# Output projection of the cross attention from split operands, split during the attention

## The chip, the cores and the metric

The program runs on one core of one Trainium2 chip. The metric is the device time of one execution in microseconds (us). Before the change the median of three runs is 2769.53 us (2766.48 to 2770.44).

## What is computed

The reference is one transformer block over x (2 x 512 tokens of 512 features): a cross attention of 16 heads against a context of 2 x 8192 tokens, a window attention, and a mixture of 16 experts with a shared feed-forward part. The change touches the last line of the first part:

```python
    out = jnp.einsum('bhqk,bhkd->bhqd', scores, v)
    out = out.transpose(0, 2, 1, 3).reshape(b, -1, N_HEADS * D_K)
    return out @ Wo.T + bo          # 1024 x 512 times 512 x 512
x = x + _L0_xattn_ref(_layernorm(x), ctx_1024, ctx_1024, mask, Wq, bq, ..., Wo, bo)
```

All of it is in fp32, and the output has to be nearly as exact as fp32.

## The kernel before, in words

TensorE takes a fp32 operand in two ways here. As plain fp32, where the profile shows two matmul records for each product, or as fp32r, a rounded form, where it shows one. Where the kernel wants the speed of fp32r and the exactness of fp32 it splits each operand: high = the operand rounded to fp32r (a ScalarE copy), low = operand minus high (a VectorE subtraction), and the product is the sum of three fp32r products, high*high, high*low and low*high. The projections of keys and values (L1896, L1908), the products of the middle stage (L1001) and those of the experts (L712, L759) are made so. The output projection (L261) is not: it multiplies plain fp32.

The program has four stages: the projection of the context in 32 chunks (to about 741 us), the attention (to 1800 us), a middle stage with the output projection, the window attention, the gate and the shared feed-forward part, and the experts.

**The attention** goes through 8 groups bg, each a batch and four heads, stacked on 128 partitions; a group goes through 64 tiles of 128 keys. For a tile TensorE makes four score products of 128 x 512 into a ring of six PSUM banks (`score`, L433), seven products ahead of their use; ScalarE takes the exponential into one of six buffers PR (`attention_scalar`, L515 one bank at a time, L519 two at a time: of the eight banks of two tiles, four go one by one and four as two pairs, so that two tiles are four L515 and two L519); TensorE multiplies by the values into bank 7 (`values`, L444); VectorE adds the tile's exponentials to one of two sums AC (`attention_vector`, L548 for the first four tiles, L552 for the others). Tiles 13, 27, 41 and 55 (`KEPT`) are not added by VectorE: TensorE multiplies them by ones (`kept_sums`, L458). A group's denominator is completed by TensorE from AC in the fifth tile of the next group (`denominator`, L460). ScalarE waits before it overwrites a buffer PR until VectorE has added the tile six before (`buffer_free`, L493). When a group is done, ScalarE copies its output from PSUM to AT (`copied_out`, L489, called at u % 128 == 2 of the next group); VectorE takes the reciprocal of the denominator and multiplies (`normal`, L528, after the eighth tile of the next group).

GpSimd does nothing in the attention: `attention_gpsimd` (L415) has two memsets, which run at 728 us. SyncE loads keys, values and queries, and WO, the output weights of 1 MB, once, at the third chunk (`attention_sync`, L400).

**The end of the attention.** The output projection has eight tiles of 128 tokens, wo0 to wo3 for batch 0 and wo4 to wo7 for batch 1, each the sum of four products over the groups of its batch (`output_projection`, L256). wo0 and wo1 come before the last group's denominator (L482, L483), wo2 and wo3 behind it; the last group belongs to batch 1, so wo4 to wo6 wait until it is normal (L1095), then come four transposes of tokens (`turn`, t20 to t23, L991), then wo7. An order written out by hand (`ORDER`, L222) gives each result one of four PSUM banks in turn: `claim` waits until the bank's last content has been taken. wo4 takes the bank of wo0, t21 to t23 those of wo4 to wo6, wo7 that of t20. VectorE takes them in this order (`middle_vector`, L1378): adds wo0 to wo3 to X with statistics between (L1388, L1391), normalises those four tiles (L1401 to L1413, with one step on GpSimd, L977), adds wo4 to wo6, subtracts for the low halves of the four transposed tiles (L1421), adds wo7. The first product of the window attention (k00, L1104) is behind wo7 on TensorE. SyncE starts to load the window weights when the last group is normal (`middle_sync`, L903).

SBUF: AT and WO are plain views of AT_R and WO_R at the same addresses. The tiles of the attention are given back at L560, and those of the middle stage take their place.

Of the kernel before, what the change touches and what calls it, by code (L numbers as in the profile page):

```python
# [22 lines left out]
F32 = mybir.dt.float32  # L23
F32R = mybir.dt.float32r
I32 = mybir.dt.int32
U32 = mybir.dt.uint32
ALU = mybir.AluOpType
ACT = mybir.ActivationFunctionType
AX = mybir.AxisListType

P = 128
B, SQ, D = 2, 512, 512
# [3 lines left out]
G = D // P  # L36
# [6 lines left out]
BG = B * G  # L43
# [25 lines left out]
def program(nc, x, ctx_t, mask, wq, bq, wk, bk, wv, bv, ident_d, blocks_d, wo, bo, pre, bqkv, wlat, blat_c,  # L69
            blat_r, wmask_d, wproj, bproj, gate_w, up_w, gw, down_w, bias_d, pick_d, sh_down, out):  # L70
    st = ExitStack()
    with st:
        def sem(name):
            return st.enter_context(nc.semaphore(name))
# [15 lines left out]
        PS = st.enter_context(nc.psum_tensor("PS", [P, 8, 512], F32))  # L90
# [40 lines left out]
        with ExitStack() as plain:  # L131
            AT = plain.enter_context(nc.sbuf_tensor("AT", [P, BG, SQ], F32))
            WO = plain.enter_context(nc.sbuf_tensor("WO", [P, G, D], F32))
# [53 lines left out]
        with ExitStack() as s1:  # L187
            def sb(name, shape, dt=F32):
                return s1.enter_context(nc.sbuf_tensor(name, shape, dt))
# [66 lines left out]
        def output_projection(pe, i):  # L256

            b, q = divmod(i, TT // B)
            bank = claim(pe, f"wo{i}")
            for g in range(G):  # L260
                m = pe.matmul(PS[:, bank, :], AT[:, g * B + b, q * P:(q + 1) * P], WO[:, g, :],  # L261
                              start=(g == 0), stop=(g == G - 1))
            m.then_inc(s_full[bank], 1)

        s_wo = sem("output_weights_in")
        s_s, s_exp, s_pv, s_acc, s_l, s_o, s_rec, s_norm = (sem(n) for n in (
            "scores_ready", "exp_ready", "tile_values_added", "sums_added",
            "denominator_ready", "output_copied", "reciprocal_ready", "output_normal"))
        GT = NCH * KT
# [44 lines left out]
        PR = [sb(f"PR{i}", [P, J, SQ]) for i in range(BUFS)]  # L314
        AC = [[sb(f"AC{x}{h}", [P, J, SQ]) for h in range(2)] for x in range(2)]
        RC = sb("RC", [P, SQ])

        def exact_max_sync(sp):
            with sp.If(sp.value_load(flag[0:1, 0:1]) == 0):
# [74 lines left out]
        def attention_sync(sp):  # L394
            for N in range(1, BG * NCH):
                bg, n = divmod(N, NCH)
                if N == 2:
                    for s in range(2):
                        sp.wait_ge(s_kvst[s], STORES * NC_ALL // 2 + 1)
                    sp.dma_start(WO[:], wo).then_inc(s_wo, 16)  # L400
                if n == 0:
                    if bg >= 2:
                        sp.wait_ge(s_s, (bg - 1) * J * GT)
                    load_queries(sp, bg % 2, bg)
                if N >= 2:
                    sp.wait_ge(s_s, (N - 1) * J * KT)
                if N >= 2:
                    load_keys(sp, N % 2, N, bg % B * NCH + n)
                if N >= 2:
                    sp.wait_ge(s_pv, (N - 1) * KT)  # L410
                else:
                    sp.wait_ge(s_vps, 2 * KT + NC_ALL * KT)
                load_values(sp, N % 2, N)

        def attention_gpsimd(pool):  # L415
            pool.wait_ge(s_kps, NC_ALL * G)
            nc.gpsimd.memset(KS[1][3 * DH:P].bitcast(F32), 1.0).then_inc(s_row, 1)
            nc.gpsimd.memset(QS[1][3 * DH:P].bitcast(F32), 0.0).then_inc(s_row, 1)

        def attention_tensor(pe):  # L420
            def score(m):
                tile, j = divmod(m, J)
                N, t = divmod(tile, KT)
                bg = tile // GT
                if m % (J * GT) == 0:
                    pe.wait_ge(s_qs[bg % 2], (bg // 2 + 1) * QSB)
                if m % (J * KT) == 0:
                    pe.wait_ge(s_kv[N % 2], (N // 2 + 1) * KVB)
                if m >= RING:
                    pe.wait_ge(s_exp, exponentials(m - RING))  # L430
                elif m >= G:
                    pe.wait_ge(s_vs, NC_ALL * KT + m - G + 1)
                pe.matmul(PS[:, m % RING, :], KS[N % 2][:, j, t * P:(t + 1) * P], QS[bg % 2][:, j, :],  # L433
                          start=True, stop=True).then_inc(s_s, 1)

            def values(tile):
                bg, q = divmod(tile, GT)
                N, t = divmod(tile, KT)
                if t == 0:
                    pe.wait_ge(s_v[N % 2], (N // 2 + 1) * 16)  # L440
                if q == 0 and bg:
                    pe.wait_ge(s_o, bg)
                for j in range(J):
                    m = pe.matmul(PS[j * DH:(j + 1) * DH, OUTB, :], VC[N % 2][:, t, j * DH:(j + 1) * DH],  # L444
                                  PR[tile % BUFS][:, j, :], start=q == 0, stop=q == GT - 1)
                m.then_inc(s_pv, 1)

            def column_sums(src, start=False, stop=False):

                for j in range(J):  # L450
                    m = pe.matmul(PS[j * DH:(j + 1) * DH, SUMB, :], ones[:], src[:, j, :], start=start, stop=stop)  # L451
                return m

            def kept_sums(bg, q):

                if q == KEPT[0] and bg:
                    pe.wait_ge(s_rec, bg)
                column_sums(PR[(bg * GT + q) % BUFS], start=q == KEPT[0]).then_inc(s_l, 1)  # L458

            def denominator(bg):  # L460

                pe.wait_ge(s_acc, (bg + 1) * MARKS)
                column_sums(AC[bg % 2][0])
                column_sums(AC[bg % 2][1], stop=True).then_inc(s_l, 1)

            for m in range(LEAD):
                score(m)
            pe.wait_ge(s_vs, (NC_ALL + 1) * KT)
            for p in range(BG * GT // 2):
                bg, q = divmod(2 * p, GT)  # L470
                for m in range(p * BATCH + LEAD, min((p + 1) * BATCH + LEAD, NM)):
                    score(m)
                pe.wait_ge(s_exp, 8 * p + 8)
                values(2 * p)
                values(2 * p + 1)
                if q + 1 in KEPT:
                    kept_sums(bg, q + 1)
                if bg and q == 4:
                    denominator(bg - 1)
            pe.wait_ge(s_wo, 16)  # L480
            pe.wait_ge(s_norm, BG - 1)
            output_projection(pe, 0)  # L482
            output_projection(pe, 1)  # L483
            denominator(BG - 1)
            output_projection(pe, 2)
            output_projection(pe, 3)

        def attention_scalar(act):
            def copied_out(bg):  # L489
                act.wait_ge(s_pv, bg * GT + GT)  # L490
                nc.scalar.activation(AT[:, bg, :], PS[:, OUTB, :], ACT.Copy).then_inc(s_o, 1)

            def buffer_free(tile):  # L493

                act.wait_ge(s_pv, tile + 1)
                bg, q = divmod(tile, GT)
                if q in KEPT:
                    act.wait_ge(s_l, summed(bg, q))
                else:
                    act.wait_ge(s_acc, added(tile))  # L500

            act.wait_ge(s_vps, 2 * KT + NC_ALL * KT)
            act.wait_ge(s_vs, (NC_ALL + 1) * KT)
            for i in range(2):
                act.wait_ge(s_qst[i], 32 * (BG // 2))
                act.wait_ge(s_pst[i], 16 * SLICES + 1)
            for u in range(NM // 2):
                tile, hp = divmod(u, 2)
                bank = 2 * u % RING
                if hp == 0 and tile >= BUFS:  # L510
                    buffer_free(tile - BUFS)
                if halved(u):
                    for jj in range(2):
                        act.wait_ge(s_s, 2 * u + jj + 1)
                        nc.scalar.activation(PR[tile % BUFS][:, 2 * hp + jj], PS[:, bank + jj, :], ACT.Exp,  # L515
                                             scale=SCALE).then_inc(s_exp, 1)
                else:
                    act.wait_ge(s_s, 2 * u + 2)
                    nc.scalar.activation(PR[tile % BUFS][:, 2 * hp:2 * hp + 2], PS[:, bank:bank + 2, :], ACT.Exp,  # L519
                                         scale=SCALE).then_inc(s_exp, 2)  # L520
                if u % (2 * GT) == 2 and u >= 2 * GT:
                    copied_out(u // (2 * GT) - 1)
            copied_out(BG - 1)

        def attention_vector(dve):
            v = nc.vector
# [26 lines left out]
                    if bg and i == 7:  # L553
                        normal(bg - 1)
            normal(BG - 1)
            dve.wait_ge(s_norm, BG)

# [342 lines left out]

        def middle_sync(sp):  # L903
            sp.wait_ge(s_norm, BG)
            for i in range(2):
                sp.wait_ge(s_pst[i], 16 * SLICES + 1)

# [76 lines left out]
        def middle_tensor(pe):  # L984
# [107 lines left out]
                                  start=(f == 0), stop=(f == FS - 1))  # L1092
                m.then_inc(s_full[bank], 1)

            pe.wait_ge(s_norm, BG)  # L1095
            for i in range(4, TT - 1):
                output_projection(pe, i)
            for i in range(4):
# [992 lines left out]
```

## Time and profile before

| what | value |
|---|---|
| median of three runs | 2769.53 us |
| profiled execution, its own time | 2769.25 us |
| its span (first to last instruction) | 2767.5 us |
| TensorE busy, share of the span | 2741.3 us, 99% |
| VectorE / ScalarE / GpSimd busy | 2197.8 / 1736.6 / 88.9 us |
| instructions | 38269 |

Times of a row are microseconds from the start of the span unless marked ns. PE is TensorE's matmul, PEld its weight load, DVE VectorE, ACT ScalarE, POOL GpSimd, SPq SyncE's DMA queue. L552 is line 552 of the kernel. A matmul is pipelined, so the mean time of one is longer than the step from one to the next. A bracket behind a row gives the time for which the engine was idle before it and what ended that.

### The profile page before, as it was taken

The page shows a single profiled execution, that of the slowest core. Times are in us where ns is not written, and L with a number is a line of the kernel's source. Part 1 is how long each engine was busy: PE and PEld are TensorE (multiplying, and loading weights), DVE is VectorE, ACT ScalarE, POOL GpSimd, SP SyncE. Part 2 cuts the span into 40 slices and gives each one's busy share as a digit, 9 for nine tenths or more (in the row PEclk, how much of TensorE's full clock was granted, in tenths as well). Part 3 has the DMA queues.
Part 4 walks back from the last instruction along what each step waited for, and adds up shares of the span by engine and source line. Part 5 has one row for each costly group of instructions (what it writes and reads, how often), then busy time and mean ns, then how long its engine had stood idle before and what let it go on. Part 6 is the DMA issues. An engine that isn't in the chain of part 4 may idle for free.

```text
span 2767.5 us, 38269 instructions
## 1 busy us (share of the span) xinstructions
PE 2741.3 (99%) x14389; PEld 1811.2 (65%) x14389; DVE 2197.8 (79%) x1645; ACT 1736.6 (63%) x2519; POOL 88.9 (3%) x43
## 2 busy tenths in 40 slices
PE   9999999999999999999999999999999999999998
PEld 5888888888744444444444444457766788888886
DVE  6545544445599999999999999967659888888886
ACT  4222222222499999999999999916531577777775
POOL 0000000000000000000000000000000400000000
PEclk9999999999999999999999999999999999999999
DMA  6666666666655555556555565430352899999995
GB/s 232 231 229 235 228 217 233 235 227 235 193 127 141 132 135 134 140 127 141 128 138 137 133 142 131 109 106 32 122 195 91 326 360 349 343 353 345 347 345 195
DMA packets 245283, 553.30 MB, mean 200 GB/s; under 512 B 19971, under 2 KB 85891, under 8 KB 215805
## 3 DMA queue, kind: packets, MB, share of 16 engines
q1 hardware_dynamic: 241548, 542.91, 61.3%
q0 software_dynamic: 3584, 8.39, 1.4%
q8 instruction: 94, 1.54, 0.2%
q14 instruction: 57, 0.46, 0.1%
HBM read 423.10 MB, written 128.12 MB: 199 GB/s over the span
## 4 chain that ended last, share of the span: by engine, by line
PE 97%; DVE 1%; DMA 1%; issue 0%; ACT 0%; POOL 0%; SPq 0%; DVEq 0%; ACTq 0%
PE PS L433 19%; PE PS L444 17%; PE PS L1908 13%; PE PS L1896 12%; PE PS L712 12%; PE PS L759 6%; PE PS L1001 6%; PE PS L1091 2%; PE PS L451 1%; PE PS L701 1%; PE PS L261 1%; PE PS L1951 1%; PE PS L1059 1%; PE PS L738 1%; PE PS L1024 1%; DMA RAW<-in_gw 1%
## 5 line engine op out<-in xcount | busy, mean ns | idle before, releaser
L552 DVE TENSOR_TENSOR AC<-AC,PR 128x2048 f32<-128x2048 f32 x448 | 988.5, 2282 | 4.8 <-ACT PR L515 4.8
L515 ACT ACTIVATE PR<-PS 128x512 f32<-128x512 f32 x1024 | 567.6, 610 | 64.7 <-PE PS L433 42.0
L433 PEld LDWEIGHTS PS<-QS,KS 128*128 128x128 f32 x2048 | 364.0, 187 | 333.1 <-ACT PR L519 182.4
L433 PE MATMUL PS<-QS,KS 128*128 128x512 f32 x2048 | 562.7, 415 | 0.8 <-ACT PR L519 0.5
L519 ACT ACTIVATE PR<-PS 128x1024 f32<-128x1024 f32 x512 | 502.4, 1051 | 0.0
L444 PE MATMUL PS<-PR,VC 128*32 128x512 f32 x4096 | 492.5, 598 | 0.7 <-ACT PR L515 0.7
L610 DVE TENSOR_TENSOR WL<-RAW,WH 128x2048 fp32r<-128x2048 f32 x192 | 436.4, 2287 | 60.2 <-ACT WH L605 60.2
L1828 ACT ACTIVATE KH<-PS,bk_s 128x512 fp32r<-128x512 f32 x128 | 88.0, 690 | 520.2 <-PE PS L1896 520.2
L605 ACT ACTIVATE WH<-RAW 128x2048 fp32r<-128x2048 f32 x192 | 362.0, 1913 | 11.6 <-PE PS L1091 5.2
L1713 DVE SCALAR_TENSOR_TENSOR KL<-PS,bk_s,KH 128x512 fp32r<-128x512 f32 x128 | 95.5, 750 | 258.4 <-ACT KH L1828 258.4
L444 PEld LDWEIGHTS PS<-PR,VC 128*32 128x32 f32 x4096 | 106.8, 109 | 216.5 <-issue 169.2
L712 PE MATMUL PS<-WL,XEH 128*128 128x512 f32 x512 | 200.5, 392 | 0.0
L712 PE MATMUL PS<-WH,XEL 128*128 128x512 f32 x512 | 200.1, 391 | 0.0
L712 PE MATMUL PS<-WH,XEH 128*128 128x512 f32 x512 | 199.6, 390 | 0.0
L1908 PE MATMUL PS<-WVH,CL 128*128 128x512 f32 x512 | 199.3, 389 | 0.1
L1908 PE MATMUL PS<-WVH,CH 128*128 128x512 f32 x512 | 199.4, 389 | 0.0
L1908 PE MATMUL PS<-WVL,CH 128*128 128x512 f32 x512 | 199.2, 389 | 0.0
L1896 PE MATMUL PS<-CH,WKH 128*128 128x512 f32 x496 | 192.9, 389 | 0.0
L1896 PE MATMUL PS<-CL,WKH 128*128 128x512 f32 x496 | 192.9, 389 | 0.0
L1896 PE MATMUL PS<-CH,WKL 128*128 128x512 f32 x496 | 192.9, 389 | 0.0
L1722 DVE TENSOR_TENSOR VS<-PS,bv_s 128x512 f32<-128x512 f32 x128 | 85.2, 686 | 84.5 <-PE PS L1908 84.5
L800 ACT ACTIVATE HTH<-PS 128x512 fp32r<-128x512 f32 x64 | 38.3, 599 | 146.8 <-PE PS L738 146.8
(244 smaller groups left out, 3366.7 us busy)
## 6 DMA issues: line engine op xcount, KB each, us to landing
KS<-kh_d SPq DMA_DIRECT2D x256, 256.0 KB
RAW<-in_gw SPq DMA_DIRECT2D x64, 1024.0 KB, 6.2
RAW<-in_up_w SPq DMA_DIRECT2D x64, 1024.0 KB, 5.7
RAW<-in_down_w SPq DMA_DIRECT2D x64, 1024.0 KB, 5.6
kh_d<-KH SPq DMA_DIRECT2D x32, 1024.0 KB, 4.4
kl_d<-KL SPq DMA_DIRECT2D x32, 1024.0 KB, 6.5
v_d<-VS SPq DMA_DIRECT2D x128, 256.0 KB, 2.9
KS<-kl_d SPq DMA_DIRECT2D x128, 256.0 KB
```

The costliest lines, as they stand in the source:

```text
L433: pe.matmul(PS[:, m % RING, :], KS[N % 2][:, j, t * P:(t + 1) * P], QS[bg % 2][:, j, :], start=True, stop=True).then_inc(s_s, 1)
L444: m = pe.matmul(PS[j * DH:(j + 1) * DH, OUTB, :], VC[N % 2][:, t, j * DH:(j + 1) * DH], PR[tile % BUFS][:, j, :], start=q == 0, stop=q == ...
L515: nc.scalar.activation(PR[tile % BUFS][:, 2 * hp + jj], PS[:, bank + jj, :], ACT.Exp, scale=SCALE).then_inc(s_exp, 1)
L519: nc.scalar.activation(PR[tile % BUFS][:, 2 * hp:2 * hp + 2], PS[:, bank:bank + 2, :], ACT.Exp, scale=SCALE).then_inc(s_exp, 2)
L552: v.tensor_tensor(a[i % 2][:], a[i % 2][:], p[:], ALU.add).then_inc(s_acc, 1)
L605: nc.scalar.activation(WH[n % PAIRS][:], RAW[:, n % RAWS], ACT.Copy).then_inc(s_hi, 1)
L610: nc.vector.tensor_tensor(WL3[n % PAIRS][:], RAW[:, n % RAWS], WH[n % PAIRS][:].bitcast(F32), ALU.subtract).then_inc(s_lo, 1)
L712: m = pe.matmul(PS[:, bank, :], x[e % 2][:, c, :], w[:, c, :], start=False, stop=i == len(terms) - 1)
L759: m = pe.matmul(PS[:, bank, :], h[S % 2][:, f, :], w[:, f, :], start=False, stop=k == FC - 1 and i == len(terms) - 1)
L1001: m = pe.matmul(PS[:, bank, :], a[:, c, f * P:(f + 1) * P], x_[:, c, :], start=(k == 0), stop=(k == len(terms) - 1))
L1896: mm = pe.matmul(PS[:, g, :], w[:, c, g * P:(g + 1) * P], a[s][:, c, :], start=(k == 0), stop=(k == len(terms) - 1))
L1908: mm = pe.matmul(PS[:, G + t, :], a[s][:, c, t * P:(t + 1) * P], w[:, c, :], start=(k == 0), stop=(k == len(terms) - 1))
```

## The change

The output projection multiplies split operands. The weights are loaded to a tile of their own, WOS, from which GpSimd makes the high half WOH (a copy) and the low half WO_R (a subtraction) early in the attention. Of each of the first seven groups ScalarE makes the high half ATH (`output_hi`, at u % 128 == 40, that is within tile 20 of the next group) and GpSimd then the low half AT_R, in place. Of the last group ScalarE makes the high half behind `copied_out`, and VectorE the low half, behind `normal` and ahead of all that it does in the middle stage. TensorE's waits before wo0 and before wo4 are for these halves. SyncE waits in `middle_sync` for the weights' low half too. Two of the new tiles, LINES5 and LINES6, are only there for the addresses.

```diff
@@ output_projection
             bank = claim(pe, f"wo{i}")
-            for g in range(G):
-                m = pe.matmul(PS[:, bank, :], AT[:, g * B + b, q * P:(q + 1) * P], WO[:, g, :],
-                              start=(g == 0), stop=(g == G - 1))
+            t = slice(q * P, (q + 1) * P)
+            terms = [(a, w) for g in range(G) for a, w in ((ATH[:, b * G + g, t], WOH[:, g, :]), (ATH[:, b * G + g, t], WO_R[:, g, :]),
+                                                           (AT_R[:, g * B + b, t], WOH[:, g, :]))]
+            for k, (a, w) in enumerate(terms):
+                m = pe.matmul(PS[:, bank, :], a, w, start=(k == 0), stop=(k == len(terms) - 1))
             m.then_inc(s_full[bank], 1)
 
-        s_wo = sem("output_weights_in")
+        s_wo, s_woh, s_wol = sem("output_weights_in"), sem("output_weights_hi"), sem("output_weights_lo")
+        s_ath, s_atl, s_atl7 = sem("output_hi"), sem("output_lo"), sem("last_output_lo")
@@ tiles of the attention
+        LINES5 = sb("LINES5", [P, 640])
+        WOH = sb("WOH", [P, G, D], F32R)
+        LINES6 = sb("LINES6", [P, 128])
+        ATH = sb("ATH", [P, BG, SQ], F32R)
+        WOS = sb("WOS", [P, G, D])
@@ attention_sync
-                    sp.dma_start(WO[:], wo).then_inc(s_wo, 16)
+                    sp.dma_start(WOS[:], wo).then_inc(s_wo, 16)
@@ attention_gpsimd
+            pool.wait_ge(s_wo, 16)
+            nc.gpsimd.tensor_copy(WOH[:], WOS[:]).then_inc(s_woh, 1)
+            pool.wait_ge(s_woh, 1)
+            nc.gpsimd.tensor_tensor(WO_R[:], WOS[:], WOH[:].bitcast(F32), ALU.subtract).then_inc(s_wol, 1)
+            for bg in range(BG - 1):
+                pool.wait_ge(s_ath, bg + 1)
+                nc.gpsimd.tensor_tensor(AT_R[:, bg, :], AT[:, bg, :], ATH[:, bg % B * G + bg // B, :].bitcast(F32), ALU.subtract
+                                        ).then_inc(s_atl, 1)
@@ attention_tensor
-            pe.wait_ge(s_wo, 16)
-            pe.wait_ge(s_norm, BG - 1)
+            pe.wait_ge(s_wol, 1)
+            pe.wait_ge(s_atl, BG - 1)
@@ attention_scalar
+            def output_hi(bg):
+                act.wait_ge(s_norm, bg + 1)
+                nc.scalar.activation(ATH[:, bg % B * G + bg // B, :], AT[:, bg, :], ACT.Copy).then_inc(s_ath, 1)
...
                     copied_out(u // (2 * GT) - 1)
+                if u % (2 * GT) == 40 and u >= 2 * GT:
+                    output_hi(u // (2 * GT) - 1)
             copied_out(BG - 1)
+            output_hi(BG - 1)
@@ attention_vector
             normal(BG - 1)
-            dve.wait_ge(s_norm, BG)
+            dve.wait_ge(s_ath, BG)
+            v.tensor_tensor(AT_R[:, BG - 1, :], AT[:, BG - 1, :], ATH[:, BG - 1, :].bitcast(F32), ALU.subtract).then_inc(s_atl7, 1)
@@ middle_sync
             sp.wait_ge(s_norm, BG)
+            sp.wait_ge(s_wol, 1)
@@ middle_tensor
-            pe.wait_ge(s_norm, BG)
+            pe.wait_ge(s_atl7, 1)
             for i in range(4, TT - 1):
                 output_projection(pe, i)
```

## Rows read from the trace of the kernel before

**Rows 1.** The page: span, and the chain that ended last by engine

```profile
span 2767.5 us, 38269 instructions
...
PE 97%; DVE 1%; DMA 1%; issue 0%; ACT 0%; POOL 0%; SPq 0%; DVEq 0%; ACTq 0%
```

**Rows 2.** Instructions of line 261: ns min/median/max, first and last start

```profile
L261 PE MATMUL PS<-WO,AT x64: 592/592/697, 1800.4 to 1832.6; 128*128 128x512 f32 x64
```

**Rows 3.** The chain in order of time, middle stage: start, us, what

```profile
1871.99 4.54 PE PS L1001 x12
1887.57 5.36 PE PS L1001 x12
...
1904.83 2.74 PE PS L1001 x12
```

**Rows 4.** Timeline at the end of the attention: start, us, engine, line

```profile
1800.44 7.13 PE L261 MATMUL PS<-WO,AT 128*128 128x512 f32 x16
...
1807.51 1.92 PE L451 MATMUL PS<-AC,ones 128*32 128x512 f32 x16
...
1809.50 3.36 DVE L532 RECIPROCAL RC<-PS 128x512 f32<-128x512 f32 x1 [4.73 <-PE PS L451]
...
1813.64 0.67 DVE L1388 TENSOR_TENSOR X<-X,PS 128x512 f32<-128x512 f32 x1
...
1826.83 0.69 DVE L1388 TENSOR_TENSOR X<-X,PS 128x512 f32<-128x512 f32 x1 [1.98 <-PE PS L261]
...
1829.50 3.70 PE L261 MATMUL PS<-WO,AT 128*128 128x512 f32 x8 [0.95 <-DVE RAW_R L1421]
```

**Rows 5.** Timeline of ScalarE about the third group's copy out

```profile
1136.91 1.96 ACT L519 ACTIVATE PR<-PS 128x1024 f32<-128x1024 f32 x2
1139.02 0.60 ACT L491 ACTIVATE AT<-PS 128x512 f32<-128x512 f32 x1
1139.51 2.06 ACT L515 ACTIVATE PR<-PS 128x512 f32<-128x512 f32 x4
...
1143.23 2.30 ACT L515 ACTIVATE PR<-PS 128x512 f32<-128x512 f32 x4
```

**Rows 6.** Timeline of the weight loads in the same stretch: first scores of three batches

```profile
1134.92 1.46 PEld L433 LDWEIGHTS PS<-QS,KS 128*128 128x128 f32 x7 [0.84 <-ACT PR L519]
...
1138.88 0.99 PEld L433 LDWEIGHTS PS<-QS,KS 128*128 128x128 f32 x5 [0.84 <-ACT PR L519]
...
1143.41 1.45 PEld L433 LDWEIGHTS PS<-QS,KS 128*128 128x128 f32 x7 [0.84 <-ACT PR L519]
```

**Rows 7.** Timeline of VectorE in the attention, groups one to three and the last

```profile
773.47 101.42 DVE L552 TENSOR_TENSOR AC<-AC,PR 128x2048 f32<-128x2048 f32 x46 [0.30 <-ACT PR L515]
875.84 2.29 DVE L548 TENSOR_TENSOR AC<-PR 128x2048 f32<-128x2048 f32 x1 [0.94 <-ACT PR L515]
879.71 2.29 DVE L548 TENSOR_TENSOR AC<-PR 128x2048 f32<-128x2048 f32 x1 [1.58 <-ACT PR L515]
...
889.35 2.29 DVE L552 TENSOR_TENSOR AC<-AC,PR 128x2048 f32<-128x2048 f32 x1 [0.74 <-ACT PR L515]
...
1021.77 2.29 DVE L552 TENSOR_TENSOR AC<-AC,PR 128x2048 f32<-128x2048 f32 x1 [0.63 <-ACT PR L515]
...
1027.98 114.59 DVE L552 TENSOR_TENSOR AC<-AC,PR 128x2048 f32<-128x2048 f32 x52
...
1690.18 114.59 DVE L552 TENSOR_TENSOR AC<-AC,PR 128x2048 f32<-128x2048 f32 x52
```

**Rows 8.** Timeline of ScalarE, exponentials of tiles 28 and 29 of that group

```profile
1063.07 1.96 ACT L519 ACTIVATE PR<-PS 128x1024 f32<-128x1024 f32 x2
```

**Rows 9.** Groups of GpSimd's own instructions, whole span

```profile
L977 POOL TENSOR_TENSOR ln_tmp<-ln_tmp,minus_half 128x4 f32<-128x4 f32 x4 | 4.1, 1022 | 1323.2 <-DVE ln_tmp L1403 1323.2
...
L417 POOL MEMSET KS<- 32x2048 f32 x1 | 1.8, 1810 | 728.1 <-PE PS L1896 728.1
```

**Rows 10.** Windows: length, then busy PE, PEld, DVE, ACT, POOL, granted clock, DMA, GB/s

```profile
1886.00:1890.00 4.00, 4.00 (x22) 3.28 (x19) 3.97 (x14) 3.19 (x17) 0.00 (x0) 0.50 0.00 0
```

## The prediction

> **What bounds the kernel now.** I read the page first: TensorE holds 97% of the chain that ended last [rows 1]. So a change pays only where TensorE, or what TensorE waits for, gets shorter. The profiled execution took 2769.25 us, its span is 2767.5 [rows 1]; the median of the three runs is 0.3 us above that, which is nothing.
>
> Then the line itself. The output projection has 64 records [rows 2], two for each of its 32 products. Its first 16 take 7.13 us [rows 4]; the last of a run shows 0.70 [rows 2], so a record steps by (7.13 - 0.70) / 15 = 0.429 us and the whole by 27.4 us. Products of split operands step by 2.74 / 12 = 0.228 us [rows 3].
>
> Then the stretch behind it, for who waits. VectorE is idle once, 1.98 us, for wo6 [rows 4], and TensorE once, 0.95 us, ahead of wo7 for VectorE's low half of t20 [rows 4]. Both engines take turns there: neither's saving comes through alone.
>
> Last the attention, where the new work is put. TensorE, ScalarE and VectorE are all nearly full in it. VectorE has its adds one behind the other, 52 in 114.59 us [rows 7], 2.20 us each; its idle times are 0.30 us in the first group, 0.94 + 1.58 + 0.74 us in the second, and 0.63 us in each of the next six [rows 7] (one of six alike stands there): 7.3 us in all.
>
> **TensorE's products.** 96 at 0.228 us are 21.9 us in place of 27.4: 5.5 us less. How much of it is kept follows from the order. wo0 and wo1 need 5.5 us in place of 6.9, so the last denominator's sums start 1.4 us earlier than 1807.51 [rows 4] and the last group is normal at 1812.2 in place of 1813.6. Now ScalarE has to copy its high half (0.60 us for such a tile, the copy out [rows 5]) and VectorE to subtract (0.67 us, as an add of that size [rows 4]); with 0.1 for the two handovers that is 1.4 us. So VectorE starts on wo0 at 1813.6, as before. What is queued behind its new wait, all of the middle stage's vector work, starts no later, but no earlier. TensorE, done with wo3 at 1813.4, waits 0.9 us for the bank of wo0, finishes wo6 at 1822.6 in place of 1826.6, and VectorE's wait of 1.98 us is gone. TensorE then waits for VectorE at t21 to t23 and again ahead of wo7, which starts 2.0 us earlier; wo7 itself is 0.7 us shorter. Less 0.1 for handovers, **the tail gains 2.6 us** of the 5.5.
>
> **Seven copies on ScalarE.** `copied_out` shows what one more copy costs in the attention. The first scores of the batches begin 3.96 us apart, and 4.53 us where the copy is [rows 6]: 0.57 us. That copy began 0.15 us behind the end of the exponentials, where the instruction after it starts 0.11 us ahead of an end, because it has to wait for TensorE; the new one waits for nothing. The copy itself takes 0.49 us of ScalarE's order (1139.02 to 1139.51), and the four exponentials behind it take 2.06 in place of 2.30 us [rows 5], since their scores are there already. So one costs between 0.49 - 0.24 = 0.25 and 0.57 us, and I take 0.4, the middle: **seven cost 2.8 us** (1.8 to 4.0). The eighth is in the tail above.
>
> **GpSimd beside VectorE.** Nine new instructions: a copy and a subtraction of 2048 elements per partition at about 752 us, and seven subtractions of 512. GpSimd itself has nothing else to do there. The question is whether VectorE, whose adds read two SBUF tiles, is held up while they run. No row shows such an overlap. If it is never held, they cost nothing. From above: GpSimd's memset moves 2048 elements in 1.81 us, and its smallest two-input instruction takes 1.02 us [rows 9]; with two or three such passes and 1.02 us to start, 4.6 + 6.5 + 7 x 2.4 = 27.9 us. I take that VectorE is held for the reads, one or two passes at the memset's rate, and 0.2 us to start each: 1.8 + 3.6 + 7 x 0.9 + 9 x 0.2 = 13.5 us of holds. [...]
>
> What do holds do? First they use up VectorE's 7.3 us of idle time. The rest makes VectorE late. That stops ScalarE only where a buffer is needed again: the fifteenth of the 52 adds, tile 23, ends at 1027.98 + 14 x 2.20 + 2.29 = 1061.1 [rows 7], and tile 29, which takes its buffer, starts with the second instruction of the row at 1063.07, at 1064.0 [rows 8]: 2.9 us of slack. At the end VectorE's last add is done at 1690.18 + 114.59 = 1804.8 [rows 7], while the denominator began at 1807.51 [rows 4]. So with H us of holds the denominator moves by H - 7.3 - 2.6, the high and low half add 1.4, the tail gives back 2.0 + 0.7: in sum H - 11.2, once that is above the floor set by TensorE and ScalarE, 2.8 - 2.6 = +0.2. With 13.5 it is **+2.3 us**; the floor holds up to H = 11.4.
>
> **The rest.** SyncE's load goes to another tile at the same place in its queue, behind the same waits. The new wait in `middle_sync` is for something done a thousand microseconds earlier. TensorE's wait for seven low halves is for the seventh, made in the eighth group's tile 20, some 85 us ahead. None costs anything as long as GpSimd gets its turn. The window weights are asked for 1.4 us earlier.
>
> **Sum.** -2.6 + 2.8 = +0.2, raised by holds to +2.3: 2771.6 on the profiled execution, 2771.8 on the median. 0.2% of this kernel is 5.5 us, about what can be told from no change.
>
> **Rivals.**
> 1. No hold-up, or under 11.4 us of it (0.20). For: no row shows one, and the idle time and buffers swallow much. Then +0.2, 2769.7; were the copies free as well, 2766.9.
> 2. Slower: VectorE becomes the bound (0.17). From H = 16.7 us, that is 0.35 us more per instruction than I take, it passes 0.2%. For: its idle time per group is only 0.63 us [rows 7]. With 20 us, +8.8: 2778.3. [...]
> 3. TensorE's clock falls ahead of wo7 (0.18). Between wo6 and wo7 it now has 5 us with only sixteen transposes. [...] Against: before, the transposes and the wait of 0.95 us did no harm. [...]
> 4. Faster (0.05): no hold-up, free copies, and the later stage falls into step so that its two slow products [rows 3] run at 2.74 us: -2.6 - 1.8 - 2.6 = -7.0, 2762.5.
> 5. The split isn't done in the attention (0.03): VectorE, always first, keeps GpSimd out, and TensorE waits at wo0 for it, some 12 us: 2781.
>
> **Chances.** The forecast has 0.37 and gives no change, with its own range from 2769.5 to 2775; faster 0.05; slower 0.23 (rivals 2 and 5, and 0.03 of rival 3); the same 0.72. The range, 2766.5 to 2778.5, takes in the free copies and half of rival 2, and leaves out 0.17.
>
> **What would show it.** Right: 96 records of line 261 at 0.228 us; batches with the new copy longer by 0.3 to 0.5 us; VectorE's adds longer than 2.29 us where GpSimd runs, its waits in the attention gone; no wait of VectorE for wo6; wo7 at about the same distance from the window products. Wrong: adds of 2.29 us throughout (rival 1), ScalarE waiting for VectorE in every group (rival 2), a granted clock under 1 from 1823 on (rival 3), or a start of wo0 put off by GpSimd (rival 5).

## The result, and the profile after

The changed kernel takes 2777.68 us (median of 8 runs, 2776.05 to 2778.93), the kernel before, run beside it, 2769.07 us (8 runs, 2766.04 to 2771.13): ratio 1.0033, 95% interval 1.0024 to 1.0042. It is slower by 8.6 us. That is inside the stated range, 0.8 us from its upper end, and outside the 2769.5 to 2775 that the forecast gave itself as no change. It got into the range by luck: the time comes from something else than the forecast added up, as the rest shows.

The page of the changed kernel: the span, each engine's busy time, the chain that ended last, and two groups of instructions.

```profile
span 2775.7 us, 38352 instructions
PE 2740.7 (99%) x14421; PEld 1818.3 (66%) x14421; DVE 2208.1 (80%) x1646; ACT 1741.1 (63%) x2527; POOL 847.0 (31%) x52
PE 93%; POOL 4%; DVE 2%; DMA 1%; issue 0%; ACT 0%; SPq 0%; DVEq 0%; ACTq 0%; POOLq 0%
...
L433 POOL TENSOR_TENSOR AT_R<-AT,ATH 128x512 fp32r<-128x512 f32 x7 | 748.6, 106948 | 300.0 <-ACT ATH L511 300.0
...
L575 DVE TENSOR_TENSOR AC<-AC,PR 128x2048 f32<-128x2048 f32 x448 | 998.3, 2306 | 0.0
```

GpSimd, absent from the chain before [rows 1], now holds 4% of it. Seven subtractions of 512 elements per partition have a mean of 106.9 us each, while VectorE's 448 adds stand at 2306 ns, hardly more than the 2.29 of [rows 7]. If one of the two engines waits for the other, it is GpSimd. GpSimd's timeline:

```profile
749.87 3.54 POOL L428 CAST WOH<-WOS 128x2048 fp32r<-128x2048 f32 x1 [17.34 <-DMA WOS<-in_wo]
753.50 6.51 POOL L430 TENSOR_TENSOR WO_R<-WOS,WOH 128x2048 fp32r<-128x2048 f32 x1
915.98 111.19 POOL L433 TENSOR_TENSOR AT_R<-AT,ATH 128x512 fp32r<-128x512 f32 x1 [155.96 <-ACT ATH L511]
1048.83 107.86 POOL L433 TENSOR_TENSOR AT_R<-AT,ATH 128x512 fp32r<-128x512 f32 x1 [21.67 <-ACT ATH L511]
...
1712.80 95.83 POOL L433 TENSOR_TENSOR AT_R<-AT,ATH 128x512 fp32r<-128x512 f32 x1 [22.65 <-ACT ATH L511]
```

The weights' subtraction is four times as large as the others and took 6.5 us. Where the others end is seen on VectorE's timeline:

```profile
1017.12 8.89 DVE L575 TENSOR_TENSOR AC<-AC,PR 128x2048 f32<-128x2048 f32 x4
1025.93 3.35 DVE L555 RECIPROCAL RC<-PS 128x512 f32<-128x512 f32 x1
...
1148.84 9.99 DVE L575 TENSOR_TENSOR AC<-AC,PR 128x2048 f32<-128x2048 f32 x4
...
1692.91 114.59 DVE L575 TENSOR_TENSOR AC<-AC,PR 128x2048 f32<-128x2048 f32 x52
1818.58 3.36 DVE L555 RECIPROCAL RC<-PS 128x512 f32<-128x512 f32 x1 [11.07 <-PE PS L467]
...
1823.36 0.69 DVE L580 TENSOR_TENSOR AT_R<-AT,ATH 128x512 fp32r<-128x512 f32 x1 [0.70 <-ACT ATH L511]
1823.99 0.67 DVE L1413 TENSOR_TENSOR X<-X,PS 128x512 f32<-128x512 f32 x1
...
1840.84 0.69 DVE L1413 TENSOR_TENSOR X<-X,PS 128x512 f32<-128x512 f32 x1 [1.32 <-PE PS L264]
```

The first subtraction ends at 1027.17, 1.2 us into the reciprocal of 1025.93, which reads PSUM. The second ends at 1156.69, within the four adds before the next reciprocal, which take 9.99 us in place of 8.89: there GpSimd got in, and one add waited 1.1 us. It is the fourth:

```profile
1153.25 2.29 DVE L575 TENSOR_TENSOR AC<-AC,PR 128x2048 f32<-128x2048 f32 x1
1155.49 3.34 DVE L575 TENSOR_TENSOR AC<-AC,PR 128x2048 f32<-128x2048 f32 x1
```

It starts 2.24 us behind the third, where the adds otherwise step by 2.20, because it had to wait for this exponential of ScalarE's, which ended 0.03 us before it (in the kernel before, the same add waits some 0.63 us [rows 7]):

```profile
1154.86 0.60 ACT L535 ACTIVATE PR<-PS 128x512 f32<-128x512 f32 x1 [1.78 <-PE PS L449]
```

The third, fourth and fifth subtractions end in the same way, the add starting 0.03 to 0.04 us behind its exponential. Where the exponential was done earlier, 1.07 us ahead of the add in the first case and 0.09 us in the sixth, GpSimd stayed out until the reciprocal. So in the second to the fifth a wait of VectorE let it in, although the profile counts almost no idle time there. The seventh was asked for at 1712.80, in the middle of 52 adds without a gap that end at 1807.5; it ends at 1808.63. TensorE's timeline at that place, and the end of the values before it:

```profile
1801.42 1.92 PE L460 MATMUL PS<-PR,VC 128*32 128x512 f32 x16 [0.69 <-ACT PR L535]
1808.77 0.76 PE L264 MATMUL PS<-WOH,ATH 128*128 128x512 f32 x1 [5.43 <-POOL AT_R L433]
1809.33 0.63 PE L264 MATMUL PS<-WO_R,ATH 128*128 128x512 f32 x1
...
1813.17 0.50 PE L264 MATMUL PS<-WO_R,ATH 128*128 128x512 f32 x1
1813.51 0.40 PE L264 MATMUL PS<-WOH,AT_R 128*128 128x512 f32 x1
...
1816.59 1.92 PE L467 MATMUL PS<-AC,ones 128*32 128x512 f32 x16
...
1837.79 0.50 PE L264 MATMUL PS<-WOH,ATH 128*128 128x512 f32 x1 [1.20 <-DVE RAW_R L1446]
```

wo0 stands for 5.43 us behind that one subtraction and starts 0.14 us after its end at 1808.63, so the late end in GpSimd's row is a real one. And then its first products are slow: nine steps from 1809.33 to 1813.17 are 0.427 us each, those behind them 0.228. The windows show the clock (length, busy time of PE, PEld, DVE, ACT, POOL, granted clock, DMA, GB/s):

```profile
1808.00:1813.00 5.00, 4.23 (x10) 3.39 (x11) 0.00 (x0) 0.00 (x0) 0.67 (x2) 0.50 0.00 0
1813.00:1825.00 12.00, 11.41 (x56) 7.70 (x56) 5.69 (x6) 0.63 (x1) 0.00 (x0) 0.98 0.10 16
```

A granted clock of 0.50 behind a wait of 5.4 us, and 0.98 in the window after that; before, wo0 came straight behind the values, with 1.00 from 1800 to 1807.

Where the time went, in times of the profiled executions, starts but for the first and the last line (before from [rows 4]; the last column is an experiment told below, in which the seventh low half is VectorE's):

| point | before | changed | seventh on VectorE |
|---|---|---|---|
| TensorE done with the values | 1800.4 | 1803.3 | 1802.5 |
| wo0 | 1800.44 | 1808.77 | 1802.53 |
| last denominator | 1807.51 | 1816.59 | 1808.19 |
| reciprocal | 1809.50 | 1818.58 | 1810.18 |
| VectorE's add of wo0 | 1813.64 | 1823.99 | 1815.59 |
| wo7 | 1829.50 | 1837.79 | 1829.38 |
| span | 2767.5 | 2775.7 | 2765.2 |

The first line is later by 2.9 us, of which 0.5 were there before the stage (VectorE's first add of the attention begins at 745.48 in place of 744.97), so the attention took 2.4. The wait is 5.4. wo0 and wo1 take 7.8 us in place of 7.1, although split products at full clock would take 5.7: the low clock cost 2.2. Copy and subtraction ahead of VectorE's add of wo0 are 1.3, which makes 10.35 there. The tail gives back 2.1 by wo7, and 0.7 in it, which leaves 7.6. The span is longer by 8.2: the other 0.6 comes behind wo7, where this profile and the one before differ in more than one place, and no experiment is about it.

### The profile page after: what moved, and what is told of

It is laid out like the page before. It is cut to its first block, busy times and chain, and to the rows that moved or that the text cites. A ratio compares the mean times of both kernels' runs of the same rounds, so it can differ in the third digit from the quotient of the medians.

```text
span 2775.7 us, 38352 instructions
## 1 busy us (share of the span) xinstructions
PE 2740.7 (99%) x14421; PEld 1818.3 (66%) x14421; DVE 2208.1 (80%) x1646; ACT 1741.1 (63%) x2527; POOL 847.0 (31%) x52
## 4 chain that ended last, share of the span: by engine, by line
PE 93%; POOL 4%; DVE 2%; DMA 1%; issue 0%; ACT 0%; SPq 0%; DVEq 0%; ACTq 0%; POOLq 0%
PE PS L449 18%; PE PS L460 16%; PE PS L1933 13%; PE PS L1921 12%; PE PS L736 12%; PE PS L783 6%; PE PS L1026 6%; POOL AT_R L433 3%; PE PS L1116 2%; PE PS L467 1%; PE PS L725 1%; PE PS L1976 1%; PE PS L1084 1%; PE PS L762 1%; DMA RAW<-in_gw 1%; PE PS L1049 1%
## 5 line engine op out<-in xcount | busy, mean ns | idle before, releaser
L575 DVE TENSOR_TENSOR AC<-AC,PR 128x2048 f32<-128x2048 f32 x448 | 998.3, 2306 | 0.0
L433 POOL TENSOR_TENSOR AT_R<-AT,ATH 128x512 fp32r<-128x512 f32 x7 | 748.6, 106948 | 300.0 <-ACT ATH L511 300.0
L719 POOL DMA_INDIRECT out<-YO,token x16 | 51.9, 3242 | 528.1 <-DVE YO L876 528.1
```

The source lines that it names most:

```text
L433: nc.gpsimd.tensor_tensor(AT_R[:, bg, :], AT[:, bg, :], ATH[:, bg % B * G + bg // B, :].bitcast(F32), ALU.subtract).then_inc(s_atl, 1)
L575: v.tensor_tensor(a[i % 2][:], a[i % 2][:], p[:], ALU.add).then_inc(s_acc, 1)
```

## The experiments

The theory, for this kernel: a GpSimd instruction that reads SBUF does not get in while VectorE's adds of two SBUF tiles follow one another without a gap. It ends in VectorE's next gap, where an add has to wait for its input, or beside the reciprocal, which reads PSUM (the first ended 1.2 us into it). Its own work is about a microsecond (1.29 us in the probe below). For six groups nobody waits for it; for the seventh TensorE does. The rivals: GpSimd is slow in itself or slowed in proportion to its size; the loss is that of the copies, or of VectorE held by GpSimd.

**Copies alone.** The kernel before, with the seven high copies, which nobody reads; the projection stays plain fp32.

```diff
+            def output_hi(bg):
+                act.wait_ge(s_norm, bg + 1)
+                nc.scalar.activation(ATH[:, bg % B * G + bg // B, :], AT[:, bg, :], ACT.Copy).then_inc(s_ath, 1)
...
+                if u % (2 * GT) == 40 and u >= 2 * GT:
+                    output_hi(u // (2 * GT) - 1)
```

> The kernel before, with ScalarE's seven high copies of tile 20 added and nothing else (nobody reads them; the projection is plain fp32). Theory A (GpSimd shut out by VectorE's adds is what costs, and the copies cost what the attention of the changed kernel is longer, 2.4 us): 2.4 us over the kernel before, batches with a copy longer by 0.34 us. Theory B (the copies are most of the loss): 5 us or more. Nothing at all (under 1 us) would say that the 2.4 us are holds of VectorE.

Measured: 2770.66 us beside 2768.18 for the kernel before (11 and 27 runs), ratio 1.0010 (1.0001 to 1.0019). Seven copies cost 2.5 us, 0.35 each; the interval alone, 0.3 to 5.3 us, would allow much less or more. The profiled execution agrees:

```profile
745.63 2.29 DVE L560 TENSOR_TENSOR AC<-PR 128x2048 f32<-128x2048 f32 x1 [4.08 <-ACT PR L525]
...
1803.53 7.13 PE L261 MATMUL PS<-WO,AT 128*128 128x512 f32 x16
```

wo0 starts 1057.90 us behind VectorE's first add of the attention, in place of 1055.47 (1800.44 - 744.97): 2.4 us. There is no work of GpSimd in this kernel's attention, so the 2.4 us are not holds of VectorE.

**Copies and GpSimd's splits.** The same, and GpSimd splits the weights and six groups into tiles that nobody reads.

```diff
+            nc.gpsimd.tensor_copy(WOH[:], WO[:]).then_inc(s_woh, 1)
...
+            for bg in range(BG - 2):
+                pool.wait_ge(s_ath, bg + 1)
...
+                nc.gpsimd.tensor_tensor(WOS[:, bg % G, :], AT[:, bg, :], ATH[:, bg % B * G + bg // B, :].bitcast(F32), ALU.subtract
+                                        ).then_inc(s_atl, 1)
```

> The same, and GpSimd's splits too, of the weights and of the first six groups, into tiles that nobody reads; the projection is plain fp32 and waits for none of it. Theory A: as c1 within 1 us, because a hold of VectorE is swallowed and a late GpSimd hurts only who waits for it; the six subtractions still last some 108 us each. Theory B (holds make VectorE the bound, rival 2 of the prediction): 4 us or more over c1, and ScalarE waits for VectorE's sums.

Measured: 2770.18 us, ratio 1.0008 (0.9999 to 1.0017), no more than the copies alone. GpSimd's timeline, its weights and the first and the last group:

```profile
752.87 6.51 POOL L428 TENSOR_TENSOR WOS<-WO,WOH 128x2048 fp32r<-128x2048 f32 x1
915.45 111.09 POOL L434 TENSOR_TENSOR WOS<-AT,ATH 128x512 fp32r<-128x512 f32 x1 [156.06 <-ACT ATH L512]
...
1579.46 107.85 POOL L434 TENSOR_TENSOR WOS<-AT,ATH 128x512 fp32r<-128x512 f32 x1 [24.96 <-ACT ATH L512]
```

The long subtractions are here too, and neither they nor what VectorE loses to GpSimd cost anything that these runs can tell. The interval ends at 4.7 us, so copies and holds together are not the 8.6 us.

**A probe.** The kernel before with one GpSimd instruction per group, into a tile that nobody reads: a memset, a copy, a subtraction of 512 elements, one of 64, a memset, and at last a subtraction meant to start with a reciprocal.

```diff
+            probes = [lambda: g.memset(PROBE[:], 1.0), lambda: g.tensor_copy(PROBE[:], AT[:, 1, :]),
+                      lambda: g.tensor_tensor(PROBE[:], AT[:, 2, :], AT[:, 1, :], ALU.subtract),
+                      lambda: g.tensor_tensor(PROBE[:, 0:64], AT[:, 3, 0:64], AT[:, 1, 0:64], ALU.subtract),
+                      lambda: g.memset(PROBE[:], 1.0),
+                      lambda: g.tensor_tensor(PROBE[:], AT[:, 3, :], AT[:, 4, :], ALU.subtract)]
```

> The kernel before with one GpSimd instruction per group from the second group on, with no reader: in tile 20 a memset of 512 elements, a copy of 512, a subtraction of 512, a subtraction of 64, a memset again, and last a subtraction of 512 started with VectorE's reciprocal. Theory A (an instruction that reads SBUF has to wait for a gap between VectorE's adds of two SBUF tiles, one that only writes doesn't): memsets 0.5 to 1 us; copy and both subtractions about 108 us, whatever their size; the one started with the reciprocal, which reads PSUM, 1.2 us. If size sets the time, that of 64 elements lasts an eighth of that of 512. [...]

GpSimd's timeline, whole attention:

```profile
920.09 0.53 POOL L422 MEMSET PROBE<- 128x512 f32 x1 [187.88 <-DVE AC L569]
1052.55 101.63 POOL L422 COPY PROBE<-AT 128x512 f32<-128x512 f32 x1 [131.93 <-DVE AC L569]
1185.00 102.31 POOL L423 TENSOR_TENSOR PROBE<-AT 128x512 f32<-128x512 f32 x1 [30.82 <-DVE AC L569]
1317.80 101.35 POOL L424 TENSOR_TENSOR PROBE<-AT 128x64 f32<-128x64 f32 x1 [30.49 <-DVE AC L569]
1449.82 0.53 POOL L425 MEMSET PROBE<- 128x512 f32 x1 [30.67 <-DVE AC L569]
1551.09 1.29 POOL L426 TENSOR_TENSOR PROBE<-AT 128x512 f32<-128x512 f32 x1 [100.74 <-DVE AC L569]
```

VectorE's timeline at the ends of the third and of the last:

```profile
1286.78 2.68 DVE L569 TENSOR_TENSOR AC<-AC,PR 128x2048 f32<-128x2048 f32 x1 [0.63 <-ACT PR L532]
...
1551.62 2.91 DVE L569 TENSOR_TENSOR AC<-AC,PR 128x2048 f32<-128x2048 f32 x1 [0.61 <-ACT PR L532]
```

An eighth of the elements takes as long (101.35 and 102.31 us), one operand as long as two (101.63), and a memset, which reads nothing, takes 0.53 us among the same adds. The third ends at 1287.31, just behind the start of the first add that follows a gap (0.63 us). The last one missed its aim: it started one add early, but in such a gap, and so shows what the instruction takes when it is let in, 1.29 us, and what VectorE then pays, an add of 2.91 in place of 2.29 us. Size and slowness of GpSimd are out. This kernel has one execution, 2765.98 us, which is no verdict on its time.

A gap of 0.63 us let the third in, and the handovers between adds that were both ready, one each 2.20 us over the 101.78 us ahead of that, did not.

**The seventh low half on VectorE.** The changed kernel, but for this. By the theory TensorE then has neither the wait of 5.43 us ahead of wo0 nor the granted clock of 0.50 behind it.

```diff
-            for bg in range(BG - 1):
+            for bg in range(6):
                 pool.wait_ge(s_ath, bg + 1)
...
-            pe.wait_ge(s_atl, BG - 1)
+            pe.wait_ge(s_atl, 6)
+            pe.wait_ge(s_atl7, 1)
...
+                    if bg - 1 in (6,) and q == 24:
+                        low_half(bg - 1)
```

> The changed kernel with the low half of the seventh group made by VectorE (in tile 24 of the last group) in place of GpSimd. [...] Theory B: VectorE gets 0.7 us more to do, so no gain: 2777 or more. The denominator should start 1.4 us sooner behind wo0 than before and VectorE should not wait for wo6.

Measured: 2768.15 us beside 2768.18 (11 and 27 runs), ratio 1.0000 (0.9991 to 1.0009). The whole slowdown is gone, within the 2.5 us that the interval leaves either way. VectorE's and then TensorE's timeline:

```profile
1727.42 0.68 DVE L563 TENSOR_TENSOR AT_R<-AT,ATH 128x512 fp32r<-128x512 f32 x1
...
1810.18 3.36 DVE L556 RECIPROCAL RC<-PS 128x512 f32<-128x512 f32 x1 [2.80 <-PE PS L467]
```

```profile
1802.53 0.50 PE L264 MATMUL PS<-WOH,ATH 128*128 128x512 f32 x1
...
1808.19 1.92 PE L467 MATMUL PS<-AC,ones 128*32 128x512 f32 x16
...
1829.38 0.50 PE L264 MATMUL PS<-WOH,ATH 128*128 128x512 f32 x1 [1.20 <-DVE RAW_R L1452]
```

VectorE does in 0.68 us what took GpSimd 95.83, and still waits 2.80 us for the denominator. wo0 follows the values at once, wo0 and wo1 take 1808.19 - 1802.53 = 5.66 us. Against the two experiments above, which have the copies but not the split products, it is less: by 2.5 us against the copies alone, by 2.0 against copies and GpSimd's splits. That is the gain of the tail.

**A gap for GpSimd.** The rest of the changed kernel as it is; in the last group VectorE waits once for the seventh low half.

```diff
+                    if bg == BG - 1 and q == 24:
+                        dve.wait_ge(s_atl, BG - 1)
```

> The changed kernel with one wait more: VectorE, ahead of the add of tile 24 of the last group plus one, waits until GpSimd has done its seventh subtraction, so that its stream of adds has one gap. Theory A (GpSimd needs a gap, not time): the seventh subtraction lasts some 10 us (the adds already queued) and not 96, VectorE stands still for 1.3 us, TensorE doesn't wait ahead of wo0, and the time is that of e1 within 1.5 us: 2768 to 2770. If GpSimd were slow in itself, VectorE would stand still for many microseconds, ScalarE for want of buffers, and the time would be above the changed kernel's 2777.7.

Measured: 2769.70 us beside 2768.37 for the kernel before (11 and 33 runs), ratio 1.0002 (0.9993 to 1.0011). GpSimd's row, and VectorE's:

```profile
1712.58 17.50 POOL L433 TENSOR_TENSOR AT_R<-AT,ATH 128x512 fp32r<-128x512 f32 x1 [25.02 <-ACT ATH L511]
```

```profile
1730.12 79.37 DVE L575 TENSOR_TENSOR AC<-AC,PR 128x2048 f32<-128x2048 f32 x36 [1.18 <-ACT PR L539]
```

The same instruction, on the same engine, beside the same neighbours, ends after 17.5 us (some 10 were expected), as soon as VectorE stands still, and VectorE stands still for 1.18 us for it (the row names ScalarE, which had long been done with that tile: the wait is the new one). An extra wait on an engine that was nearly full removed the slowdown. This settles the mechanism: the wait was for VectorE's adds and not for GpSimd's work. The two experiments take away the wait and the low clock behind it together, so the 2.2 us of the clock are read from the timeline alone.

**The copies in ScalarE's idle time.** As with the seventh on VectorE, and each high copy at tile 29, between two exponentials where ScalarE stands idle for TensorE; VectorE's subtraction for the seventh group moves from tile 24 to tile 40, to be behind its copy. The idle time in the kernel before:

```profile
1066.43 1.58 ACT L515 ACTIVATE PR<-PS 128x512 f32<-128x512 f32 x3 [0.92 <-PE PS L433]
```

```diff
+                        if jj and u % (2 * GT) == 59 and u >= 2 * GT:
+                            output_hi(u // (2 * GT) - 1)
...
-                if u % (2 * GT) == 40 and u >= 2 * GT:
-                    output_hi(u // (2 * GT) - 1)
```

> e1 with the seven high copies moved from tile 20 to tile 29, between ScalarE's two single exponentials there, where it is idle for 0.92 us behind the sums of a kept tile. If ScalarE's order sets the price of a copy: the 2.4 us of c1 go, 2765.5 to 2766.5. If TensorE's turns set it, no change against e1's 2768.2.

Measured: 2766.45 us, ratio to the kernel before 0.9994 (0.9984 to 1.0003). ScalarE's timeline in the second group:

```profile
1065.25 0.67 ACT L512 ACTIVATE ATH<-AT 128x512 fp32r<-128x512 f32 x1
1066.32 1.58 ACT L538 ACTIVATE PR<-PS 128x512 f32<-128x512 f32 x3 [0.41 <-PE PS L449]
```

ScalarE waits 0.41 us behind the copy: the copy fits. wo0 starts 2.45 us sooner than with the copies at tile 20 (1800.08 in place of 1802.53), and the last denominator 1.83 us sooner (1806.36 in place of 1808.19), since TensorE now waits for VectorE's last add. The medians, each against the kernel before of its round, say 1.9 us. TensorE's timeline:

```profile
1806.36 1.92 PE L467 MATMUL PS<-AC,ones 128*32 128x512 f32 x16 [0.55 <-DVE AC L580]
```

**All seven low halves on VectorE**, the copies as in the last one; the edit is `(0, 1, 2, 3, 4, 5, 6)` for `(6,)`, and GpSimd's loop over the groups goes.

> e3 with all seven low halves on VectorE, so that GpSimd only splits the weights. VectorE gets 0.61 us per group and is spared a hold of 1.1 us per group; its idle time of 0.63 us per group is what pays. Expected: as e3 within 0.5 us. If VectorE becomes the bound, up to 0.6 us per group more, 4 us over e3.

Measured: 2766.22 us, 0.9994 (0.9985 to 1.0003), the same as with six on GpSimd. Its profiled execution shows something else. The windows about wo7, in this kernel and then in that of the last experiment (six on GpSimd):

```profile
1825.00:1832.00 7.00, 5.24 (x19) 3.93 (x20) 4.62 (x8) 1.75 (x3) 0.00 (x0) 0.77 0.94 317
```

```profile
1825.00:1832.00 7.00, 5.24 (x25) 4.10 (x24) 5.61 (x9) 1.40 (x3) 0.00 (x0) 1.00 0.93 301
```

The same products on TensorE, waits before them that differ by less than 0.1 us, and a mean granted clock of 0.77 in one and 1.00 in the other: from the fourth product of wo7 on, a product takes 0.427 us. This is the fall of the clock that rival 3 names. It isn't there in the profile of the changed kernel (a granted clock of 1.00 from 1837 to 1842, with wo7 at 1837.79), and the medians of the two experiments do not differ by it.

**The last low half behind VectorE's add of wo0**, on the kernel with the copies in the idle time.

```diff
-            low_half(BG - 1)
...
+                    if name == "wo0":
+                        dve.wait_ge(s_ath, BG)
+                        v.tensor_tensor(AT_R[:, BG - 1, :], AT[:, BG - 1, :], ATH[:, BG - 1, :].bitcast(F32), ALU.subtract).then_inc(s_atl7, 1)
```

> e3 with the last low half made behind VectorE's add of wo0 in place of ahead of it, in the time in which VectorE waits for ScalarE's high copy (0.70 us in e1). All that follows on VectorE starts 0.6 us sooner and wo7 with it: 0.6 us under e3. If TensorE is held by the later low half ahead of wo4, nothing is gained.

Measured: 2766.49 us, 0.9994 (0.9985 to 1.0003). wo7 starts at 1826.93 in place of 1827.56, 0.6 us sooner, as meant; the median does not move by it, and 0.6 us is a quarter of what the interval can tell.

The best three are 1.9 to 2.2 us under the kernel before in their medians, and each interval reaches 1.0003. None is shown to be faster.

## Why the prediction was right in its range and wrong in its mechanism, point by point

**The number.** 2777.68 us lies between 2766.5 and 2778.5, but the upper part of the range was there for holds of VectorE (rival 2), which cost nothing that the runs can tell. The time comes from rival 5, which the range left out and whose wait was priced at more than twice what it is. That is luck; by its working the prediction was wrong.

**The step that failed** is the one that closes the part on the rest: "TensorE's wait for seven low halves is for the seventh, made in the eighth group's tile 20, some 85 us ahead. None costs anything as long as GpSimd gets its turn." It doesn't get its turn. Behind this stands the model of the holds, "I take that VectorE is held for the reads": in it only VectorE waits. It went that way for a moment in six of GpSimd's nine instructions (the weights' two held an add by 1.7 and 4.4 us, the second to the fifth of the groups' by 1.1), not at all in the other three, and in the groups only after GpSimd had waited; the duration that mattered was that wait. [Rows 7] had what decides: 52 adds in 114.59 us leave no gap, and the only idle time in a group, 0.63 us, is before the last add ahead of the reciprocal. Read with the question "when does GpSimd get in?", they give the end of each subtraction: for six groups the next group's eighth tile, for the seventh the end of the adds, at 1690.18 + 114.59 = 1804.8 and later by the copies, behind the time at which wo0 wants to start.

**Rival 5** was this, with a chance of 0.03. I priced its wait at 12 us; it is 5.4, since GpSimd needs 1.3 us once it is in, and the adds end only some 4 us behind the values. Its condition, VectorE "always first", is right for a row of adds and wrong for the gaps. The 12 us had no rows behind them.

**GpSimd beside VectorE**, which raised the sum from +0.2 to +2.3: nothing that can be told (2770.18 us with the splits, 2770.66 without). The weights' splits came where VectorE had just caught up, and the adds held by them fell into idle time. No run shows the terms of the 13.5 us of holds, one or two passes at the memset's rate and 0.2 us to start each; the profile of the changed kernel shows holds of 1.7, 4.4 and four times 1.1 us, 10.5 in all.

**The copies, +2.8.** 2.5 measured by the medians and 2.4 in the profile, 0.35 each in place of 0.4: right.

**The tail, -2.6.** Right in its size and in its parts. In the kernel with the seventh on VectorE the denominator comes 5.66 us behind wo0 in place of 7.07 (1.4, as said), VectorE's add of wo0 13.06 in place of 13.20 (no gain there, as said), wo7 26.85 in place of 29.06 (2.2, said 2.0), and the runs give 2.0 to 2.5 in all. VectorE's 1.98 us for wo6 is gone, and TensorE waits 0.59 us for the bank of wo0 (said 0.9).

**TensorE's products.** 0.228 us at full clock, as said; ten of the 96 ran at 0.427. Rival 3 has the fall of the clock at wo7, where it did not come in the changed kernel, and rival 5 has none at wo0, where it came and cost 2.2 us on top of the 5.4. [Rows 3] and [rows 10] had the size: 5.36 us in place of 2.74 for twelve products, at 0.50.

**The sum.** +0.2 for copies and tail is what the kernel with the seventh on VectorE shows (-0.03 us, interval -2.5 to +2.5). The changed kernel is at +8.6. Wait and low clock are 7.6; the other 1.0 is less than the intervals leave open. The chances were wrong by the one mechanism: a chance of 0.03 for it, when a row of the trace showed 52 adds without a gap, was too little.

## What to carry to other kernels

Two engines need not take turns. Where VectorE's adds of two SBUF tiles followed one another without a gap here (52 in 114.59 us), GpSimd's subtractions waited for the first gap or the reciprocal, up to 111.19 us for some 1.3 us of work, so such a duration is to be read from the gaps in the busy engine's timeline and not from its size. That is harmless until somebody waits for it: ask of each moved instruction where the last gap ahead of its consumer is. Where there is none, do it on the busy engine itself (0.68 us here), or give that engine a short wait (1.18 us here).

## What was not expected of the hardware

- A GpSimd subtraction of 128x64 lasted 101.35 us, one of 128x512 102.31, and 1.29 us where it met a gap; a memset among the same adds 0.53 us. The profile counts the waiting as busy time: GpSimd's 847.0 us hold, by an estimate from the 1.29 us, some nine microseconds of work in the groups' subtractions (7 x 1.3), and no view shows a wait of it for VectorE.
- GpSimd was let in where VectorE's next add started 0.03 us behind the end of the exponential that it waited for, a wait that the profile shows as 0.04 us at most, and kept out where that exponential had ended 0.09 us before the add.
- A wait of 5.43 us of TensorE was followed by ten products at a granted clock of 0.50, 0.427 us each. Waits of 0.5 to 1.2 us among the transposes ahead of wo7 were followed by the full clock in the changed kernel (1.00 from 1837 to 1842) and by the low one in one experiment (0.50 from 1829 to 1832), at the same distance from each other. What decides between them stays open.
